# A two-layer residual kernel: rounded token blocks of rows 2 to 7 kept in DRAM from the first phase, and TensorE's loop begun at step 4

## The reference

```python
# x: (8 rows, 512 tokens, 256); cond_8: (8, 8)
def _gemma_mlp(x, gate_w, up_w, down_w):              # 256 -> 1024 -> 256
    g = einsum('bsh,hi->bsi', x, gate_w); u = einsum('bsh,hi->bsi', x, up_w)
    return einsum('bsi,ih->bsh', gelu(g, approximate=True) * u, down_w)
# layer 0: two of eight experts per row, and a shared expert
w, sel = top_k(softmax(cond_8), 2); w = w / w.sum(-1)
x = x + sum_k w[:, k] * _gemma_mlp(x, expert sel[:, k]) + _gemma_mlp(x, shared_gate, shared_up, shared_down)
# layer 1: a linear layer with a low-rank part weighted by cond_8
x = x + x @ W_base.T + b_base + 2 * sum_e cond_8[:, e] * (x @ As[e].T) @ Bs[e].T
```

## Time and profile before

| | us |
|---|---|
| median of 3 runs | 809.85 |
| fastest of the 3 | 806.36 |
| the profiled execution | 810.33 |
| its span in the trace | 808.5 |

### The profile page before, as it was taken

The page is one execution under the profiler, slowest core; times in us unless marked ns, Lnnn a source line. Parts: engine busy times, 40 slices in busy tenths (PEclk is TensorE's granted clock), DMA queues, the critical chain, the costliest instruction groups (busy, mean ns, idle before and its releaser), DMA issues.

```text
span 808.5 us, 13442 instructions
## 1 busy us (share of the span) xinstructions
PE 796.3 (98%) x4140; PEld 685.2 (85%) x4140; DVE 694.0 (86%) x916; ACT 486.4 (60%) x743; POOL 316.6 (39%) x308
## 2 busy tenths in 40 slices
PE   9999999999999999999999899999989999999998
PEld 7888888888888888888888789888878888898887
DVE  4886987987877899989989798998978999899886
ACT  6564554654654556666666566666756666675663
POOL 1441321321110773465246346425624632653520
PEclk9999999999999999999999999999999999999999
DMA  7340521303214422353163245316324522632400
GB/s 207 78 115 15 155 66 21 112 0 105 92 39 123 149 81 79 112 163 118 40 195 100 78 128 150 100 63 173 116 84 126 148 79 88 176 100 68 130 2 27
DMA packets 120160, 80.86 MB, mean 100 GB/s; under 512 B 62480, under 2 KB 115472, under 8 KB 120080
## 3 DMA queue, kind: packets, MB, share of 16 engines
q1 hardware_dynamic: 120080, 79.88, 33.9%
HBM read 67.28 MB, written 12.58 MB: 99 GB/s over the span
## 4 chain that ended last, share of the span: by engine, by line
PE 92%; DVE 5%; issue 2%; ACT 0%; POOL 0%; DVEq 0%; POOLq 0%; ACTq 0%
PE ps_ring L757 57%; PE ps_acc L757 33%; DVE inner_lo L1432 1%; DVE xc L1432 1%; DVE wide L1432 1%; PE ps_ring L877 1%; DVE post L1697 1%; DVE post L1757 0%; PE ps_acc L965 0%; DVE sh_dn L1432 0%; PE ps_acc L985 0%; PE ps_acc L871 0%; PE ps_ring L775 0%; DVE stage L1831 0%; ACT post L1322 0%
## 5 line engine op out<-in xcount | busy, mean ns | idle before, releaser
L757 PE MATMUL ps_ring<-xc,wide 128*128 128x512 f32 (+1 forms) x1938 | 421.9, 366 | 6.4 <-issue 4.6
L757 PEld LDWEIGHTS ps_ring<-xc,wide 128*128 128x128 f32 x1938 | 340.8, 189 | 68.2 <-issue 5.5
L1086 ACT CAST inner_hi<-post 128x512 fp32r<-128x512 f32 x192 | 117.7, 620 | 111.5 <-DVE post L1757 38.8
L757 PE MATMUL ps_acc<-inner_hi,wide 128*128 128x512 f32 x504 | 171.3, 390 | 0.0
L1432 DVE TENSOR_TENSOR inner_lo<-post,inner_hi 128x512 fp32r<-128x512 f32 x192 | 152.5, 802 | 8.6 <-ACT inner_hi L1086 5.7
L1089 ACT ACTIVATE post<-ps_ring 128x512 f32<-128x512 f32 (+1 forms) x125 | 67.8, 545 | 93.5 <-PE ps_ring L757 92.1
L757 PEld LDWEIGHTS ps_acc<-inner_hi,wide 128*128 128x128 f32 x504 | 94.9, 188 | 19.2
L757 PE MATMUL ps_acc<-inner_lo,wide 128*128 128x512 f32 x252 | 98.5, 391 | 0.0
L1089 ACT ACTIVATE post<-post 128x256 f32<-128x256 f32 (+1 forms) x98 | 53.8, 563 | 65.0 <-DVE post L1706 46.5
L637 POOL TENSOR_TENSOR post<-post 128x512 f32<-128x512 f32 x24 | 31.0, 1292 | 135.4 <-DVE post L1484 135.4
L757 PE MATMUL ps_acc<-inner_hi,sh_dn 128*128 128x512 f32 x256 | 83.9, 389 | 0.0
(11 more groups left out here) (128 smaller groups left out, 1040.4 us busy)
## 6 DMA issues: line engine op xcount, KB each, us to landing
raw<-n_L_cond_skill_gate_dram SPq DMA_DIRECT2D x32, 256.0 KB, 3.0
raw<-in_L_cond_skill_up_dram SPq DMA_DIRECT2D x32, 256.0 KB, 3.5
raw<-n_L_cond_skill_down_dram SPq DMA_DIRECT2D x32, 256.0 KB, 3.8
xbuf<-n_L_cond_skill_gate_dram SPq DMA_DIRECT2D x32, 256.0 KB, 3.0
xbuf<-in_L_cond_skill_up_dram SPq DMA_DIRECT2D x32, 256.0 KB, 3.5
xbuf<-n_L_cond_skill_down_dram SPq DMA_DIRECT2D x32, 256.0 KB, 3.7
xt_scratch<-xbuf SPq DMA_DIRECT2D x8, 512.0 KB, 3.1
sh_scratch<-stage SPq DMA_DIRECT2D x8, 512.0 KB, 2.7
```

The lines of the kernel that those rows point to most:

```text
L757: last = pe.matmul(dst, left_[a], right_[b], start=start and n == 0, stop=stop and n == len(PASSES) - 1, skip_group_check=adds)
L1086: return nc.scalar.copy(dst, src)
```

## The change

In the first phase, from q = 1 on, the two block columns become the token halves (256 tokens) of both rows side by side (`xh`, `both`), instead of one row each. So T1 to T4 no longer mix rows, and they and B11, B21, B22 are the values that the second phase needs for each of the two rows. SP stores each quad's seven blocks and both parts to a new DRAM tensor (`store_rights`), row by row, and a row ahead of their use loads them (`load_rights`, three DMAs a row). POOL's, ACT's and DVE's sums of x for rows 2 to 7 go, and of x only the second half of the first channel block (B12, 256 columns) is still split there. ACT's cast of B11 moves from the end of unit j = 0 to the middle of unit j = 1, since it needs both rows. In row 0 the addition of `w_eff` moves from step 9 to behind step 10. PE's loop body starts at step 4 of the odd row: steps 0 to 3 of row 1 stand ahead of the loop, and those of the next odd row close the body.

```diff
+    TURN_STEP = 4
+        rights_dram = nc.dram_tensor("rights_scratch", [B - 2, P, 2 * NP * HS], F32, kind="Internal").ap()
+        def xh(c, h):
+            return xbuf[:, 0:4 * S].rearrange("p (r c h t) -> p r c h t", r=2, c=HC, h=2)[:, :, c, h, :]
...
+            def store_rights(q):
+                sp.wait_ge(right_ready, rights(q, NP))
+                sp.wait_ge(right_hi, rights(q, NP))
+                v = xc[q % 2].bitcast(F32).rearrange("p (n r t) -> p n r t", r=2, t=HS)
+                for r in range(2):
+                    sp.dma_start(rights_dram[2 * q - 2 + r].rearrange("p (n t) -> p n t", t=HS), v[:, :, r, :])\
+                        .then_inc(rights_stored, 16)
+            def load_rights(b, par):
+                v = rights_dram[b - 1].rearrange("p (l n t) -> p l n t", l=2, n=NP)
...
+                sp.dma_start(x_to[:, :, 0, :], v[:, :, B11, :]).then_inc(rights_landed, 16)
+                sp.dma_start(x_to[:, :, 2:4, :], v[:, :, B21:B22 + 1, :]).then_inc(rights_landed, 16)
+                sp.dma_start(sums_x_all(1 - par)..., v[:, :, T1:T4 + 1, :]).then_inc(rights_landed, 16)
...
+                store_rights(qn)
...
-            sp.dma_start(xf_first, xt_dram[0]).then_inc(x0_landed, 16)
+            sp.dma_start(xf_first, xt_dram[0]).then_inc(rights_landed, 16)
...
+                if not first and not last:
+                    sp.wait_ge(ex_product, (b * NS - 1) * NP)
+                    load_rights(b, par)
...
-                    G.tensor_tensor(t_a, xt(1, 0), xt(0, 0), ALU.subtract).then_inc(t_made, 1)
+                    G.tensor_tensor(both(t_a), xh(0, 1), xh(0, 0), ALU.subtract).then_inc(t_made, 1)
...
-                if not last:
-                    if not first:
-                        pool.wait_ge(out_landed, b * 128)
-                    pool.wait_ge(ex_t_ready, b + 1)
-                    sums_of_x(b + 1)
+                if first:
+                    pool.wait_ge(ex_t_ready, 1)
+                    sums_of_x(1)
...
-            def row(b, par, first):
-                pe.wait_ge(x_ready, b + 1)
-                for k in range(K):
+            def row(b, par, first, steps=range(K)):
+                for k in steps:
+                    if k == 0:
+                        pe.wait_ge(x_ready, b + 1)
+                        if not first:
+                            pe.wait_ge(rights_landed, b * 48 - 32)
...
             row(0, 0, True)
+            pe.wait_ge(ex_t_ready, 2)
+            row(1, 1, False, range(TURN_STEP))
             with pe.Fori(0, (B - 2) // 2) as i:
-                row(i * 2 + 1, 1, False)
+                row(i * 2 + 1, 1, False, range(TURN_STEP, K))
                 row(i * 2 + 2, 0, False)
-            row(B - 1, 1, False)
+                row(i * 2 + 3, 1, False, range(TURN_STEP))
+            row(B - 1, 1, False, range(TURN_STEP, K))
...
-                if more and j == 1 and q == 0:
-                    split_right(qn, B11, xt(0, 0))
+                if more and j == 1:
+                    split_right(qn, B11, xh(0, 0))
...
                 if u == NU - PAIRS:
-                    act.wait_ge(x0_landed, 16)
+                    act.wait_ge(rights_landed, 16)
+                    act.wait_ge(rights_stored, 64)
                     take_hi(x_cur(0, 0), xf_first).then_inc(x_hi, 1)
...
-                    if k == T_STEP and not last:
-                        split_sums_x(b + 1, 1 - par, first)
+                    if k == T_STEP and first:
+                        split_second_sums_x()
...
-                        take_hi(x_cur(1 - par, 0), xf).then_inc(x_hi, 1)
+                            take_hi(x_cur(1 - par, 0)[:, HS:S], xf[:, HS:S]).then_inc(x_hi, 1)
```

More of the change, by code:

```diff
@@ L208, in sums_x, with sums_x_all @@
             return sh_dn[:, 2048 + hl * 1024:2048 + (hl + 1) * 1024]
+        def sums_x_all(par):
+            return xc[1][:, 0:2048] if par == 0 else sh_dn[:, 2048:4096]
         def sums_w(n_s, hl):
@@ L553, in store_blocks, with row @@
                             .then_inc(out_landed, 16)
-            def row(b, first, last):
+            def row(b, par, first, last):
+                if not first and not last:
+                    sp.wait_ge(ex_product, (b * NS - 1) * NP)
+                    load_rights(b, par)
                 if first:
@@ L1116, in split_right @@
                                     if qn > 2 else 8 * PAIRS)
+                    if qn == Q - 1:
+                        act.wait_ge(rights_stored, 32)
                 if qn > 0 and n in (B11, B21, B22):
-                    act.wait_ge(xt_in, 4 * (qn - 1) + (1 if n == B11 else 2 if n == B21 else 4))
-                take_hi(right(qn, 0, n), src).then_inc(right_hi, 1)
+                    act.wait_ge(xt_in, 4 * (qn - 1) + (3 if n == B11 else 4))
+                    take_hi(both(right(qn, 0, n)), src).then_inc(right_hi, 1)
+                else:
+                    take_hi(right(qn, 0, n), src).then_inc(right_hi, 1)
             def split_routed_gu(b, s, j, freed, count):
@@ L1252, in _ @@
                 if more and j == 2:
-                    split_right(qn, B22, xt(1, 1))
+                    split_right(qn, B22, xh(1, 1))
                 inner_part(u, 1)
-                if more and j == 0:
-                    split_right(qn, B11, xt(0, 0))
                 if more and j == 1:
-                    split_right(qn, B21, xt(0, 1))
+                    split_right(qn, B21, xh(1, 0))
                     act.wait_ge(t_made, 4 * q + 1)
@@ L1449, in split_right @@
                 dve.wait_ge(right_hi, done)
-                take_lo(right(qn, 1, n), src, right(qn, 0, n)).then_inc(right_ready, 1)
+                if qn > 0 and n in (B11, B21, B22):
+                    take_lo(both(right(qn, 1, n)), src, both(right(qn, 0, n))).then_inc(right_ready, 1)
+                else:
+                    take_lo(right(qn, 1, n), src, right(qn, 0, n)).then_inc(right_ready, 1)
             def turn_x(qn, r):
@@ L1608, in _ @@
                     split_sums(PAIRS - 1)
-                if more and j == 1:
-                    split_right(qn, B11, xt(0, 0), rights(qn, 1))
                 if more and j == 2:
-                    split_right(qn, B21, xt(0, 1), rights(qn, 2))
+                    split_right(qn, B21, xh(1, 0), rights(qn, 2))
                     split_right(qn, T1, t_a, rights(qn, 3))
@@ L1642, in _ @@
                         split_sums(u)
+                if more and j == 1:
+                    split_right(qn, B11, xh(0, 0), rights(qn, 1))
                 if j == 0:
@@ L1739, in row @@
                             ex_seven(b, par, k, SEVEN.index(k // 2))
+                            if k == W_EFF_FIRST_STEP and first:
+                                fold_sum()
                             if k in split_at:
```

79 lines of the change are left out of this document (51 added, 28 removed).

## The result

| us | before | after |
|---|---|---|
| median | 809.88 | 800.62 |
| lowest and highest | 806.36 to 810.19 (5 runs, without the one of 4542.35) | 799.63 to 802.68 (6 runs) |
| the profiled execution | 810.33 | 802.68 |
| its span | 808.5 | 800.9 |

The ratio is 0.9899, with a 95% interval of 0.9876 to 0.9922. The forecast was 807.0 us with a range from 800.8 to 811.8: the time is just under its lower end, beside the 801.3 of rival A. The sum was made against the profiled execution; from profile to profile the change is −7.65 us where −3.3 was forecast. The profiled execution of after is the slowest of its six runs, 2 us above their median, so what follows shows the change at its least.

What follows compares the result with a forecast made beforehand. PE was taken to bound the kernel. From the profiled execution: 810.33 − 0.8 (stalls) − 1.9 (clock) − 1.7 (step 14) + 1.1 (x of row 0) = 807.0 us, range 800.8 to 811.8.

Steps and rivals of the forecast that it cites:

- rival A: At PE's loop jumps: the stall goes altogether, the target at hand or work ahead enough; 801.3 us, chance 0.13.
- What bounds the kernel: Whole kernel: PE, busy 98%, sets the time; its two loop jumps cost 8.4 us, 4.6 stall and 3.8 slow clock.
- The base: Sum starts from the profiled 810.33 us; fastest run, 4.0 us below the median, read as clock not falling after stalls.
- The loop's place: PE's jump moved to step 4: stall of 6.1 us less 4.19 in hand, 1.9 each, 0.8 us saved over two.
- The clock: Behind PE's two jumps: the clock falls after one of two shorter stalls; 1.9 us saved, bounds 0 and 3.8.
- Step 14: Rows 1 to 6: without DVE's subtraction at step 13, PE's 0.28 us delay at k = 14 goes; 1.7 us saved.
- x of row 0 behind the stores: Unit 12: row 0's x fetch queues behind quad 3's stores and PE waits; 1.1 us lost, ends 0 and 10.
- Rival C: Unit 12: stores at half the loads' rate delay row 0's x, PE stands about 11 us; 818.8 us, chance 0.08.
- What I had at nothing: ACT's B11 cast in unit j = 1, loads of rights, PE's wait for them, work off POOL and ACT: no time.
- D: Rows: DVE sets the pace, so its saved time, over 10 us, is the gain; about 799 us, chance 0.02.
- E: Jumps and step 14: the stall is no shorter and the 0.28 us turns up elsewhere; 811.4 us, chance 0.13.
- B: At the jumps: clock never or always falls after the shorter stall; 805.1 or 808.9 us, chance 0.64 together with the forecast.

Runs made afterwards that it cites:

- padded kernels: Kernels with idle instructions ahead of PE's first work, shifting its later code; such as before with 96 semaphore increments, 816.49 us, or with 80 met waits, 809.72 us.
- 12 transposes: The kernel before with 12 instead of 20 warming transposes ahead of its first real work: 807.31 us, ratio 0.9987.
- after with 72 more: The changed kernel, loop at step 4, with 72 increments of an unused semaphore ahead of PE's first wait: 818.82 us, ratio 1.0147.

## Why the prediction was wrong, and where it was right

**What bounds the kernel.** Right: PE end to end, the two jumps as the waits of size, each 2.3 us of stall and 1.9 of clock. Both are gone in after at 4.24 and 4.2 us, as worked out ahead.

**The base.** Half right in its reading of the spread. I took the fastest run, 4 us lower, as a clock that does not fall after a stall. That does happen: behind the stalls of 2.66 and 1.73 us of two traces the clock stayed at 1.00, and before has runs near 807.7 us at a mean clock of 1.0. But the 30 packets of one kernel show one jump held and one missed, and before has runs of 803, with no room for any stall. The base is a mixture of both, and the spread of 4 us allowed for a stall that does not occur, which I left out.

**The loop's place: the step that failed.** I wrote that the stall is a fixed 6.1 us from the last wait, less the work in hand, because two jumps agreed within 0.07 us, and that "the new place has nothing else different". Two jumps of one program to one target are not two independent cases: they share the alignment of the body, which is what decides. The forecast was −0.8 us for the stalls; measured −4.6. The padded kernels show the cause: stalls leave at step 0, and come back at step 4 (5.0 and 2.0 us for the two jumps), by a shift alone. Nor is the distance fixed where there is a stall: from the end of `ex_v` to PE's restart it is 6.21 and 5.77 us with 12 transposes, 6.99 and 5.77 us in after with 72 more, 7.41 us in after with the loop at step 0. At step 4 that makes stalls of 3.04 and 1.73 us, where 1.9 was forecast for both. What varies less is the time from the first packet of a missed jump to the restart: 4.3 to 4.9 us for the nine misses in the traces (451.07 to 455.64 us in before).

The Trainium skill (Runtime: NRT & Kernel Launch, Instruction fetch mechanics) says that PE's instruction memory takes 2048 instructions, eight blocks of 16 KB refilled as a queue, and that a taken branch whose target is not in a window of two pages forces a fetch. In this case's traces the first half agrees: packets are 16 KB, and a body of seven blocks is run three times with the blocks of one turn (in after, the last fetch in the loop starts at 453.3 us and the next, past its exit, at 739.0). The window of two pages does not agree: the target was 6.3 blocks back and was held. I had quoted the rule as one of the jump wherever it stands; its condition, whether the target is held, I did not work out, though the size of the body was to be had from the order.

**The clock.** The size was wrong by half, −1.9 forecast and −3.8 measured, since there was no stall for it to follow. That it falls after some stalls only was right: where the stalls are back at step 4 it fell behind the first (3.04 us) and not behind the second (1.73), one of two as forecast. But the length of the stall, from which I argued, does not decide it: it fell behind 2.00, 2.28, 2.35 and 2.43 us and stayed high behind 2.66.

**Step 14.** The mechanism was right, its size off: −1.7 forecast (6 × 0.28), −2.2 measured (6 × 0.37), over the bound of 2.0 that I had set. I had taken the distance at k = 2, 0.72 us, as what is left without the hold. The timeline of after at the same product:

```profile
450.22 0.68 DVE L1761 TENSOR_TENSOR post<-ps_ring,post 128x512 f32<-128x512 f32 x1
...
450.58 0.88 PE L808 MATMUL ps_ring<-xc,wide 128*128 128x256 f32 x6
451.30 0.88 PE L808 MATMUL ps_ring<-xc 128*128 128x256 f32 x6
452.02 0.88 PE L808 MATMUL ps_ring<-xc,wide 128*128 128x256 f32 x6
```

DVE starts the addition 1.80 us ahead of the last product, and all three stand at 0.72 us. So the product's start won its 0.28; the other 0.09 a row lie in the product itself, whose six matmuls take 0.88 us here and 0.98 in the earlier trace rows, where the weight load was held. The sum left that term out, though the row showed it.

**x of row 0 behind the stores.** Right in mechanism and size: the cast began at 198.29, between the 197.5 and 199.4 that I had given for x; PE waited 0.94 us in one execution, where 1.1 was taken, and not at all in the next. The stores' traffic:

```profile
183.00:197.00 14.00, 1.00 0.99 318
```

From 183 to 197 us all 16 DMA engines were 0.99 busy at 318 GB/s with stores and loads together. Most of these 4.45 MB, up to 3.67, are the stores, so stores in 1 KB pieces are no slower here than the 220 to 286 GB/s of the loads in the earlier trace rows. Rival C is out. Not foreseen was that SP itself is held: its issue of x took 5.89 us behind the two stores.

**What I had at nothing.** Units 6 and 10 lost 0.4 us: DVE's rest of B11, moved to the end of j = 1, stands just ahead of its additions for the unit behind (at 101.21 us in after) and makes them late. In row 0 1.0 us was lost at steps 6, 10 and 14, of which 0.6 goes with x issued first; the rest I did not trace. The cast of B11 in unit 5 fitted as forecast, with 0.17 us left where I had 0.2:

```profile
91.03 0.62 ACT L1144 CAST xc<-xbuf 128x512 fp32r<-128x512 f32 x1 [0.73 <-DVE xbuf L1526]
91.82 1.27 ACT L1222 COPY post<-ps_ring 128x512 f32<-128x512 f32 x2 [0.17 <-PE ps_ring L808]
```

The loads of the rights, PE's new wait for them, and the work taken from POOL and ACT came to nothing, as forecast.

**The rivals.** A took place, with the reason that I gave it ("the jump's target being at hand"), and I gave it 0.13 where the spread of before and the loop's entry called for more. D is out: DVE lost 20.9 us of work (694.0 to 673.1) and the time moved by the 2.2 of step 14. E and B are out, since after has no stall. That the time came so near the range is owed to A's place in it, not to the sum.

**Still open.** The offset of the loaded program; why a body that reaches a little past an edge (some 16 to 54 instructions for before, by the offset) is missed in some executions only; what decides whether the clock falls behind a stall; and the losses of row 0 at steps 6 and 14.

## What to carry to other kernels

A hardware loop whose body nearly fills an engine's instruction memory costs a whole stall and often a slow clock a jump, or nothing, by where its first instruction falls in a block of 256: count the instructions, look at the packets of the engine's instruction queue, and try a shift before anything is read into the place of the loop. A kernel whose runs lie in groups hints at this ahead: look for the event whose price is their distance. Padding for such a shift is not free where the engine is the bound; move the loop's start by real work, as this change does, or put the work that is not urgent ahead of it.

## What the runs showed of the hardware that was not expected

A body of some 1620 instructions, 6.3 blocks, is kept whole by PE over a jump: no fetch for 285 us. When it reaches into an eighth block, as I count them, a jump can take nine packets more; the profiles show a wait of 1.7 to 3.0 us for it. In seven single stalls of four traces the clock fell behind five, at a cost of about 1.9 us each, and stayed high behind two, of 1.73 and 2.66 us.

On PE an increment of a semaphore took 0.10 to 0.11 us (72 in 7.4 us, 96 in 10.6), an instruction that only waits for what is already so about 0.06 us (80 in 4.6 and in 5.1 us); both left the clock low behind them, at a further 1.4 to 2.5 us.

SP's issue of a DMA of 512 KB took 5.89 us (5.88 in a second trace) where two stores of together 3.67 MB in pieces of 1 KB were ahead of it, with the DMA engines 0.99 busy; without these stores ahead of it, it took 0.34.
